# The two matmuls on constants at the end of each layer norm of a four-layer vision tower

## The reference, cut to what matters

```python
def _layernorm(x, axis=-1, eps=1e-05):
    m = jnp.mean(x, axis=axis, keepdims=True)
    v = jnp.var(x, axis=axis, keepdims=True)
    return (x - m) / jnp.sqrt(v + eps)
...
    h = _L0_tok_ref(x, L0_tok_W, L0_tok_b)
    h = h + _L0_attn_ref(_layernorm(h, axis=-1), ...)
    h = h + _L0_ffn_ref(_layernorm(h, axis=-1), ...)
```

## Time and profile before

| | |
|---|---|
| median of 3 runs | 1077.01 us (1073.15 to 1079.69) |
| the profiled execution, its own time | 1074.89 us |
| its span, first to last instruction | 1073.1 us |
| mean granted TensorE clock | 0.876 of full speed |
| busy: PE, DVE, POOL, ACT | 84%, 41%, 31%, 29% |

### The profile page before, as it was taken

How to read it: one execution, slowest core, us unless ns; L and a number is a source line. 1 busy time by engine, 2 the same in 40 slices (tenths; PEclk the granted TensorE clock), 3 DMA queues, 4 the chain that set the end, 5 groups by cost and what they waited for, 6 DMA issues and landing times. The chain is left out here.

```text
span 1073.1 us, 18222 instructions
## 1 busy us (share of the span) xinstructions
PE 897.4 (84%) x5969; PEld 710.9 (66%) x5969; DVE 441.0 (41%) x1153; ACT 307.6 (29%) x647; POOL 334.1 (31%) x373
## 2 busy tenths in 40 slices
PE   6887999787888887998888999998895386778684
PEld 4565899474576557777576999997665365556462
DVE  1234222322152158999482222221417926444342
ACT  2221122223344135443310222221332230323321
POOL 0002455000003218885013444443000001656650
PEclk9977899798769999999899999999986585879886
DMA  9215699100000042220043889998400004746653
GB/s 371 80 42 176 210 307 316 40 1 1 1 2 2 1 159 59 59 60 1 25 174 112 295 303 311 314 318 261 98 1 1 2 2 148 251 151 210 206 142 94
DMA packets 47378, 142.35 MB, mean 133 GB/s; under 512 B 6995, under 2 KB 11222, under 8 KB 47062
## 3 DMA queue, kind: packets, MB, share of 16 engines
q1 hardware_dynamic: 37846, 117.66, 32.3%
q0 software_dynamic: 9472, 23.93, 8.2%
HBM read 128.07 MB, written 13.50 MB: 132 GB/s over the span
## 5 line engine op out<-in xcount | busy, mean ns | idle before, releaser
L1168 POOL DMA_INDIRECT L_xr<-x_rows_L,L_rows_in x96 | 93.6, 975 | 42.2 <-issue 24.3
L1793 DVE TENSOR_TENSOR L_act<-L_hid,bank 116x512 f32<-116x512 f32 (+1 forms) x56 | 35.8, 640 | 155.8 <-ACT L_hid L1762 155.8
L1682 POOL DMA_INDIRECT y_rows_L<-L_yb,L_rows_out x56 | 55.7, 995 | 101.5 <-ACT L_yb L1768 94.9
L1762 ACT ACTIVATE L_hid<-bank 116x512 f32<-116x512 f32 (+1 forms) x56 | 31.3, 559 | 152.8 <-PE bank L1732 152.8
L1726 PE MATMUL bank<-L_xtb,L_w 128*116 128x128 f32 (+1 forms) x464 | 59.2, 282 | 0.0
L1070 POOL TENSOR_TENSOR ssm_w_low<-ssm_wbc,ssm_w_high 128x512 fp32r<-128x512 f32 x24 | 49.0, 2040 | 31.8 <-ACT ssm_w_high L1035 31.8
L1488 POOL COPY L_xrow<-L_xrow 96x384 f32<-96x384 f32 x3 | 1.5, 498 | 181.4 <-ACT L_xrow L1472 181.4
L1726 PEld LDWEIGHTS bank<-L_xtb,L_w 128*116 128x116 f32 (+1 forms) x464 | 56.6, 192 | 0.0
L1117 DVE TENSOR_TENSOR_SCAN ssm_state<-ssm_decay,ssm_drive 128x576 f32<-128x576 f32 x24 | 55.5, 2312 | 0.8
L228 PE MATMUL bank<-par_const 128*128 128x512 f32 x72 | 48.3, 800 | 0.8 <-issue 0.8
L987 PE MATMUL bank<-ssm_x_high,ssm_w_high 128*128 128x288 f32 x96 | 35.1, 365 | 13.0 <-DVE ssm_out L1122 8.8
(11 more groups left out here) (440 smaller groups left out, 2000.9 us busy)
## 6 DMA issues: line engine op xcount, KB each, us to landing
L_w<-in_L2w SPq DMA_DIRECT2D x20, 696.0 KB, 5.6
L_more<-in_L2w SPq DMA_DIRECT2D x20, 696.0 KB, 5.6
L_w<-in_L2w SPq DMA_DIRECT2D x20, 384.0 KB, 7.2
L_more<-in_L2w SPq DMA_DIRECT2D x20, 384.0 KB, 7.8
L_w<-in_L0w SPq DMA_DIRECT2D x12, 576.0 KB, 4.7
L_more<-in_L0w SPq DMA_DIRECT2D x12, 576.0 KB, 5.3
ssm_wbc<-in_wBC SPq DMA_DIRECT2D x24, 256.0 KB, 2.6
L_w<-in_L3w SPq DMA_DIRECT2D x16, 384.0 KB, 3.7
```

What stands on the lines that cost most here:

```text
L1168: pool.indirect_dma_start(self.xr[j][:, :], None, self.x_rows[:, :], bass.IndirectOffsetOnAxis(ap=at, axis=0))\
L1682: pool.indirect_dma_start(X.y_rows[:, :], bass.IndirectOffsetOnAxis(ap=rows_out[h][:, j:j + 1], axis=0), y[s + j][:, :], None).then_inc(st ...
L1762: act.activation(hid[j][:, :, :], cols(gate_bank[j % 2][0:N, 0:C * R], C), ACT.Silu).then_inc(acted, 1)
L1793: dve.tensor_tensor(act_out[j][:, :, :], hid[j][:, :, :], cols(up_bank[j % 2][0:N, 0:C * R], C), ALU.mult)\
```

## The change

The second number of `LN_WARM`, the count of matmuls at L292, becomes 0. The call with the first number stays, and so does everything else.

```diff
-LN_WARM = (1, 2)
+LN_WARM = (1, 0)
```

## The result

The changed kernel is slower: 1089.25 us median of 4 runs (1086.08 to 1091.43), against 1078.12 for the kernel before in the same comparison; ratio 1.0095, 95% interval 1.0059 to 1.0131. Run again later it gave 1088.85 us and 1.0094 (1.0059 to 1.0130). Ratios are formed from the undisturbed runs of both kernels in one comparison and are not the quotients of the two medians. The forecast was 1079 with a range of 1070 to 1086, so the time lies above it.

The account below looks back on a forecast made before the run. The prediction took TensorE, busy 84% of the span, and its clock to bound the kernel. Losses of 18.8 us against a gain of 17.1 gave +1.7 on 1077.0, rounded to 1079, range 1070 to 1086.

Parts of the forecast that it names:

- inside the scan: Scan after L2a_ln: only its start was priced, as one of the dense stages at 2.0 us; nothing further inside.
- The direct gain of 17.1 us: Ends of nine layer norms: the waits for unread matmuls on constants disappear, 17.1 us together; b_ln gains nothing.
- That the clock falls in the layer norm and that the constants hand it back: Layer norm ends: clock drops to 0.50 after one-column matmuls; without constants the next stage pays 1.56 to 2.51 us.
- The price of dense stages: Dense matmuls after L0a, L1a, b_lnf, L2a, L2f, L3a: each loses 2.0 us starting at low clock, 12.0 together.
- The routings, L0f 0.5 and L3f 0.6: Routings after L0f and L3f: short 16-column matmuls and transposes lose only 0.5 and 0.6 us.
- A layer norm at the low clock: b_ln, following L1f_ln: beginning at 0.50 instead of 1.00 costs it 2.2 us.
- b_ln's 2.0 us: The 8 instructions after b_ln: at the low clock they lose 2.0 us, against no direct gain.
- The router, +1.5: Short products of the router after b_ln: a moved low stretch costs 1.5 us, bounds -2 to +4.
- The slower rival: Router after b_ln decides: no product there runs at 1.00, and dense stages lose 2.51 each; 1084 us, chance 0.20.
- The whole-gain rival: All next stages: clock returns without the constants or the loss is hidden, 17.1 us gain stays; 1060 us, chance 0.10.

Follow-up runs that it names:

- e9: The changed kernel run again, constants left out in all ten layer norms: 1088.85 us, ratio 1.0094 to the kernel before.
- e5: The changed kernel plus two unread VectorE products after each layer norm's last multiply, in place of the constants: 1099.53 us, ratio 1.0198.
- e4: The kernel before with four matmuls on constants at the end of every layer norm instead of two: 1087.39 us, ratio 1.0093.
- e6: The changed kernel with the variance matmuls making 64 equal output columns instead of one: 1065.35 us, ratio 0.9898 to the kernel before.
- e11: The kernel before with the constants left out only ahead of the routings (L0f, L2f, L3f): 1080.79 us, ratio 1.0027.
- e1: The kernel before, unchanged, run again to see how two executions differ: 1079.01 us, ratio 1.0009.
- e12: The kernel before with the constants left out only in L1f_ln, b_ln and b_lnf: 1079.19 us, ratio 1.0023.
- e14: The changed kernel with 64-column variance matmuls, as e6, once more with more rounds: 1065.12 us, ratio 0.9870 to the kernel before.

## Why the prediction was wrong, point by point

One execution of a kernel differs from the next by several us, so I set the forecast's terms beside both traces of the changed kernel, and beside the mean of the two less the mean of the two of before. All in us; a minus is a gain.

| term of the forecast | forecast | first trace | e9 | mean of two |
|---|---|---|---|---|
| direct gain, nine layer norms | -17.1 | -17.2 | -10.8 | -15.0 |
| b_ln's beginning | +2.2 | +2.1 | +2.7 | +2.4 |
| six dense stages | +12.0 | +14.0 | +11.5 | +12.4 |
| inside the scan | 0 | +1.9 | +1.8 | +1.9 |
| routings of L0 and L3 | +1.1 | +3.5 | +5.7 | +4.9 |
| b_ln's product and the router (2.0 + 1.5) | +3.5 | -1.3 | +3.8 | +0.9 |
| sum of these | +1.7 | +2.8 | +14.8 | +7.5 |
| all other stretches | 0 | +9.8 | -0.9 | +3.2 |
| span | +1.7 | +12.6 | +13.9 | +10.7 |

The first trace and e9 are compared with the first trace of before. The mean of two agrees with the medians, which say +11.

*The direct gain of 17.1 us* was right for the waits: each next stage starts 0.3 us after the last needed instruction at all nine ends where there was a wait, and in the first trace nine layer norms are 93.5 - 76.3 = 17.2 us shorter. It was too large for the layer norms as a whole, as said below.

*That the clock falls in the layer norm and that the constants hand it back* was right, and is shown: e5 (time alone does not), e4 (two are enough), e6 (with no fall there is nothing to hand back).

*The price of dense stages, 6 x 2.0 = 12.0 us,* was about right: 14.0 and 11.5 us, 12.4 in the mean of two. A single stage can pay more than the upper end of 2.51, which came from a projection of 5.02 us at 0.50: stages here stood at 0.50 for up to 6.05, and one lost 3.4. The scan's own 1.8 to 1.9 us were not counted at all: I stopped at the first copy of x.

*The routings, L0f 0.5 and L3f 0.6,* is the step that failed, and the largest error of the sum: 1.1 us forecast, 3.5 and 5.7 measured. I read two rows of 2.18 us for the 24 matmuls with 16 columns as "short, so they do not care". Both rows were at the full clock. At 1.2 GHz the same 24 instructions of the changed kernel take 3.76 and 3.82 us, and the transposes 2.13:

```profile
78.95 3.76 PE L1383 MATMUL bank<-par_L0a,xn 96*96 96x16 f32 x24 [1.11 <-PEq L242]
82.55 2.13 PE L1388 MATMUL bank<-par_const,xn 96*96 96x96 f32 x12
...
891.39 3.82 PE L1383 MATMUL bank<-par_L3a,xn 96*96 96x16 f32 x24 [1.11 <-PEq L242]
```

Their weight loads follow the same clock: one of these took 0.165 us in the trace of before and 0.280 here (medians of 24). By place the routings lost 1.7 and 1.8 us in the first trace, 3.8 and 1.9 in the second. e11 shows the group of three as a loss by itself, 1.0027 (1.0005 to 1.0050), where my terms for it made a gain of some 2 us (5.2 - 0.5 - 2.0 - 0.6).

*A layer norm at the low clock* was counted only for b_ln's beginning (2.2 us; measured 2.1 and 2.7). That the small variance matmuls can fall into a low stretch too was missing. In the second trace of the changed kernel (e9) it happened in L1a_ln and in L3a_ln, and their 24 instructions, 2.12 us elsewhere, took 3.89; here L1a_ln:

```profile
208.82 3.89 PE L282 MATMUL bank<-par_const,L1a_ln_sq 96*96 96x1 f32 x24
212.57 2.21 PE L288 MATMUL bank<-par_const,L1a_ln_inv 96*96 96x96 f32 x12
```

So in e9 the nine layer norms gained only 93.5 - 82.7 = 10.8 us. Not all of that belongs to the change: in e1, the kernel before, L1a_ln's variance matmuls took 3.89 us as well, and against e1 the gain in e9 is 12.9 us. At least one layer norm like this stands in eight of the 13 traces with one-column matmuls, in places with and without the constants, and in none of the four with 64 columns (2.8 us at most). What decides where it falls was not tried.

*b_ln's 2.0 us* was right. The first row answers to the earlier trace rows, at the low clock now; the second is the router's last product, which answers to the earlier trace rows:

```profile
262.33 4.18 PE L362 MATMUL bank<-b_yr,par_L1f 96*128 96x288 f32 x8 [4.46 <-PEq L242]
...
275.91 4.11 PE L362 MATMUL bank<-b_h,par_L1f 64*128 64x288 f32 x16 [0.84 <-PEq L346]
```

*The router, +1.5,* goes both ways, as its bounds said. In the first trace its last product, 7.80 us before, ran at the full clock in 4.11, so the stretch is 1.3 us shorter in spite of b_ln's 2.0; in e9 that product took 8.01 us and the stretch is 3.8 us longer. Against the two traces of before, the mean of two is 0.9 us where the forecast had 3.5.

*The slower rival* had the right sign and the wrong place: it asked that the router decide. Its condition was met in e9, where the clock stood at 0.50 from 257.6 to 291.7 and no product of the router ran at 1.00; that cost 3.8 us with b_ln's product, of the 13.9 us by which e9's span is longer. In the first trace it was not met, and the kernel was as slow. Even the rival's 1084 lies below the 1089 measured. e12, which holds the router, was clear of zero in neither direction.

*The whole-gain rival* is excluded by the result, by e5 and by the clock at the starts of the stages. The rule of the Trainium skill weighed in the forecast ("TensorE: Matmul & The Clock Gate", Part 1: activity releases the throttle) agrees with e4, where the product after L1a_ln took 7.97 us, and with e5, where it took 9.47 after 3.03 us without work. The closing table of that page of the Trainium skill ("Why this matters for your kernels"), which names idle gaps as what loses the clock, does not cover this case: the clock fell after a stretch in which TensorE was recorded as busy throughout, and with wider matmuls and more idle time (1.11 us in e6) it did not fall. The measurement decides.

Adding up, in the mean of two the priced places make +7.5 us instead of +1.7. The difference of 5.8 is +3.8 from the routings, +2.1 from the layer norms, +1.9 inside the scan, +0.4 and +0.2 from dense stages and b_ln's beginning, and -2.6 from the router. The other 3.2 us lie in code that the change does not touch, most of it in the end of the scan, 8.61 us in the first trace and 5.46 in the other three, and in the L2 expert blocks. Two traces of each kernel cannot tell whether that is chance; why unchanged code varies was not tried. So of the 9.0 us between the forecast's +1.7 and the +10.7 of the traces the priced places explain 5.8, and the rest stays open.

## What to carry to other kernels

Matmuls on constants that nobody reads are not waste by being unread: ask what clock the next stage starts with, and price the stage at both levels before cutting them. But they are a repair; first look at what lets the clock fall. Here the matmuls bound by their weight loads took 64 output columns instead of one at almost no cost in time, and that kept the clock up for the first 8 us behind six of the ten layer norms (e6, e14), after which the repair could go: 0.9870 of the time before (0.9858 with b_ln's two kept), against 1.0095 for cutting the repair alone. And before a small matmul is priced as insensitive, look for it once at each level of the clock.

## What the runs showed of the hardware that I had not expected

Matmuls with 1, 16 or 64 output columns, which take 0.09 us each at the full clock (24 of them 2.12, 2.18 and 2.17 us), are slowed by the low clock nearly as much as wide ones: 24 with one column 2.12 to 3.89 us, 24 with 16 columns 2.18 to 3.76 us, against 2.15 to 4.13 us for 8 with 288 columns. TensorE can lose the clock while it is recorded as busy all the time: it did at 209.95 in L1a_ln of the kernel before, after the matmuls with one column, and with 64 columns it did not fall there. A better mean clock is no measure of success: e4 had 0.888 and 1087 us, the kernel before 0.876 and 1078.
